# Attention with a row maximum sent unnegated, and the last denominators inverted in the output stage

## The reference

```python
x = x + L0(x, cond)                          # state-space layer, not touched
# L1(x, styles), 16 heads of width 32:
q, k, v = heads(q_flat), heads(k_flat), heads(v_flat)   # projections of the normalised x
attn = einsum('bhqd,bhkd->bhqk', q, k) * scale
attn = softmax(attn, axis=-1)
out = einsum('bhqk,bhkd->bhqd', attn, v).reshape(B, S, H)
out = einsum('bsh,oh->bso', out, w_weight) * w_dc[:, None, :]
skip = einsum('bsh,oh->bso', v_flat, u_weight) * u_dc[:, None, :]
return x + out + skip
```

## Time and profile before

| | |
|---|---|
| median of 3 runs | 3419.26 us (3412.98 to 3421.17) |
| the profiled execution | 3420.78 us, of it span 3419.0 us |
| mean granted TensorE clock | 0.906 of full speed |
| TensorE busy | 3041.7 us, 89% of the span |
| VectorE busy | 2272.5 us, 66% |
| ScalarE busy | 1125.7 us, 33% |
| GpSimd busy | 1132.0 us, 33% |
| DMA | 420.83 MB, mean 123 GB/s |

### The profile page before, as it was taken

The page is one execution under the profiler, slowest core; times in us unless marked ns, Lnnn a source line. Parts: engine busy times, 40 slices in busy tenths (PEclk is TensorE's granted clock), DMA queues, the critical chain, the costliest instruction groups (busy, mean ns, idle before and its releaser), DMA issues. The chain is left out here.

```text
span 3419.0 us, 55607 instructions
## 1 busy us (share of the span) xinstructions
PE 3041.7 (89%) x20298; PEld 1427.7 (42%) x20298; DVE 2272.5 (66%) x3150; ACT 1125.7 (33%) x1944; POOL 1132.0 (33%) x462
## 2 busy tenths in 40 slices
PE   6888865599999999999966999977999999999979
PEld 2555554234444444444434666652332333322324
DVE  3766763488898898989834433437767777776614
ACT  3644542011111111111112212214655665655620
POOL 0111111113333333333302110004656666666630
PEclk9878865588999999999996999988999999998989
DMA  2233224535555555555533433345424344353354
GB/s 74 114 109 142 89 104 137 131 82 141 146 149 146 149 148 147 156 144 147 144 122 125 155 116 139 128 153 127 102 56 109 93 98 106 81 125 81 75 189 144
DMA packets 248555, 420.83 MB, mean 123 GB/s; under 512 B 51736, under 2 KB 117912, under 8 KB 242024
## 3 DMA queue, kind: packets, MB, share of 16 engines
q1 hardware_dynamic: 202344, 385.61, 39.1%
q10 hardware_dynamic: 46080, 33.57, 4.7%
HBM read 257.82 MB, written 160.98 MB: 122 GB/s over the span
## 5 line engine op out<-in xcount | busy, mean ns | idle before, releaser
L491 DVE CUSTOM_DVE_ANT_0 b_h<-b_h,b_bx,b_bounds_all 128x256 f32<-128x256 f32 x2048 | 966.0, 535 | 137.9 <-PE b_bx L604 137.8
L1348 POOL TENSOR_TENSOR e_pair_sum<-e_probs 128x2048 f32<-128x2048 f32 x128 | 585.8, 4576 | 509.7 <-PE e_banks L1203 294.5
L1211 DVE TENSOR_REDUCE e_half_max<-e_banks 128x4 f32<-128x2048 f32 x256 | 585.5, 2291 | 251.0 <-PE e_banks L1164 250.9
L1324 ACT ACTIVATE e_probs<-e_banks 128x512 f32<-128x512 f32 x1024 | 556.0, 595 | 409.8 <-PE e_banks L1178 409.8
L1178 PE MATMUL e_banks<-e_qs,e_ks 97*128 97x512 f32 x1024 | 395.5, 467 | 8.7 <-DMA e_qs<-e_neg_t 4.8
L614 PE MATMUL b_y_psum<-b_h,b_c_weights 128*32 128x128 f32 x8224 | 344.2, 287 | 3.3 <-ACT b_y_stage L654 3.3
L604 PE MATMUL b_bx<-b_x_moving,b_b_weights 24*128 24x512 f32 x1024 | 265.6, 514 | 54.0 <-DMA b_x_moving<-xn_parts 44.6
L1178 PEld LDWEIGHTS e_banks<-e_qs,e_ks 97*128 97x128 f32 x1024 | 160.1, 195 | 355.6 <-ACT e_probs L1324 295.2
L654 ACT COPY b_y_stage<-b_y_psum 128x128 f32<-128x128 f32 x256 | 68.1, 266 | 724.0 <-PE b_y_psum L614 721.4
L525 PE MATMUL b_gate<-b_w_gate,b_x_tile 128*128 128x512 f32 x512 | 302.4, 674 | 3.6 <-DMA b_w_gate<-in_w_in_t_dram 3.6
L1188 PE MATMUL e_banks<-e_probs,e_v 128*32 128x512 f32 x2048 | 291.7, 643 | 0.5 <-ACT e_probs L1324 0.4
(11 more groups left out here) (183 smaller groups left out, 3358.1 us busy)
## 6 DMA issues: line engine op xcount, KB each, us to landing
b_x_moving<-xn_parts SPq DMA_DIRECT2D x256, 128.0 KB
e_ks<-qk_parts SPq DMA_DIRECT2D x48, 512.0 KB, 7.8
e_qs<-qk_parts SPq DMA_DIRECT2D x96, 256.0 KB, 11.6
xn_full<-a_xn SPq DMA_DIRECT2D x32, 512.0 KB, 2.6
xn_parts<-a_hi SPq DMA_DIRECT2D x64, 256.0 KB, 2.4
xn_parts<-a_lo SPq DMA_DIRECT2D x64, 256.0 KB, 2.4
b_x_moving<-xn_parts SPq DMA_DIRECT2D x256, 64.0 KB
silu_gate<-b_sg ACTq DMA_DIRECT2D x64, 256.0 KB, 4.1
```

The lines of the kernel that those rows point to most:

```text
L491: return nc.vector._custom_dve(bass.dve_ops.TENSOR_ADD_SAT, **operands)
L1211: nc.vector.tensor_reduce(out=half_max[:, u // UNITS % 2, :, r // NH, r % NH], in_=(banks[:, u % 2 * GROUP:(u % 2 + 1) * GROUP] if u < FIR ...
L1324: nc.scalar.activation(probs[:, g % 4, h, :], p_exp[h % 2], ACT.Exp).then_inc(exps, 1)
L1348: nc.gpsimd.tensor_tensor(out=pair_sum[:, t % 2], in0=probs[:, (2 * t) % 4], in1=probs[:, (2 * t + 1) % 4], op=ALU.add).then_inc(paired, 1)
```

## The change

In the attention stage the negation and its semaphore go. The transpose writes `max_t`, and `send_max` sends that; the 97th row of the stacked keys is -1 where it was 1. The wait for the buffer's earlier sends moves from the negation to the transpose. `invert` stays for batches 0 to 2. For the last batch VectorE only waits for the key sums in the attention stage. The PSUM tensor is now allocated around both stages: the output stage inverts the denominators straight out of its eighth bank, as VectorE's first operation, and SyncE stores them there. The output stage's SyncE asks for x2 of 3 tiles, then batch 1, then waits for the reciprocal and stores it, and only then asks for the other five x2 and batches 2 and 3.

```diff
 def send_max(sp, m):
-            sp.wait_ge(max_row, START + m + 1)
+            sp.wait_ge(max_turned, START + m + 1)
...
-                sp.dma_start(dst.bitcast(f32), neg_t[half][block * 32:block * 32 + ROWS, :].bitcast(f32)).then_inc(max_in[half], 16)
+                sp.dma_start(dst.bitcast(f32), max_t[half][block * 32:block * 32 + ROWS, :]).then_inc(max_in[half], 16)
...
 def dve_row(dve, m):
...
-            nc.vector.transpose(max_t[half][:], row_max[half][:]).then_inc(max_turned, 1)
-            dve.wait_ge(max_turned, START + m + 1)
             if m >= 2:
                 dve.wait_ge(max_in[half], START + m // 2 * SENDS)
-            nc.vector.tensor_scalar(out=neg_t[half][:], in0=max_t[half][:], scalar1=-1.0, scalar2=None, op0=ALU.mult).then_inc(max_row, 1)
+            nc.vector.transpose(max_t[half][:], row_max[half][:]).then_inc(max_turned, 1)
...
                 store_o(sp, HALVES - 1)
-                store_rden(sp, BATCH - 1)
                 for i in range(SLOTS):
                     sp.wait_ge(raw_out[i], START + 16 * ((HALVES - 1 - i) // SLOTS + 1))
-                sp.wait_ge(rden_out, START + BATCH * RDENS)
+                sp.wait_ge(rden_out, START + (BATCH - 1) * RDENS)
...
-                    nc.vector.memset(ks[i][KROWS:STACK].bitcast(f32), 1.0).then_inc(cleared, 1)
+                    nc.vector.memset(ks[i][KROWS:STACK].bitcast(f32), -1.0).then_inc(cleared, 1)
...
-                invert(dve, BATCH - 1)
+                dve.wait_ge(key_sums, START + BATCH * LANES * NQ)
...
 def out_phase
-        po = [ctx.enter_context(nc.psum_tensor(f"f_po{i}", [P, MODEL], f32)) for i in range(4)]
+        po = [banks[:, i] for i in range(4)]; den = banks[:, 7]; rden = sb("rden", [P, 512])
...
-                for t in range(NQ):
+                for t in range(3):
                     load_x2(sp, t)
-                for b in range(1, BATCH):
-                    load_batch(sp, b)
+                load_batch(sp, 1)
+                sp.wait_ge(inverted, START + 1)
+                for h in range(P // HD):
+                    sp.dma_start(RD[BATCH - 1, h], rden[h * HD:h * HD + NH * NK, :]).then_inc(rden_out, 16)
+                for t in range(3, NQ):
+                    load_x2(sp, t)
+                load_batch(sp, 2)
+                load_batch(sp, 3)
+                sp.wait_ge(rden_out, START + P // HD * 16)
                 load_rd(sp, BATCH - 1)
...
+                nc.vector.reciprocal(out=rden[:], in_=den).then_inc(inverted, 1)
                 for t in range(TILES):
```

More of the change, by code:

```diff
@@ L1056, in _, with attention_phase @@
                 batches(dve, body)
-def attention_phase(nc, I, QK, V, OT, RD, WDC, w_out, w_row, mats):
+def attention_phase(nc, I, QK, V, OT, RD, WDC, w_out, w_row, mats, banks):
     GROUP = P // HD
@@ L1082, in attention_phase @@
         sb = lambda n, s, d=f32: ctx.enter_context(nc.sbuf_tensor("e_" + n, s, d))
-        pb = lambda n, s, d=f32: ctx.enter_context(nc.psum_tensor("e_" + n, s, d))
         sems = []
@@ L1096, in attention_phase @@
         max_t = [sb(f"max_t{i}", [P, 32]) for i in range(2)]
-        neg_t = [sb(f"neg_t{i}", [P, 32], f32r) for i in range(2)]
         probs = sb("probs", [P, 4, GROUP, HALFQ]); pair_sum = sb("pair_sum", [P, 2, GROUP, HALFQ])
         raw = sb("raw", [P, SLOTS, HALFQ]); rden = sb("rden", [P, HALFQ]); den = sb("den", [P, HALFQ]); rd = sb("rd", [P, 2, HALFQ])
-        banks = pb("banks", [P, 2 * GROUP, 512])
         p_max = banks[:, 0:GROUP]; p_exp = [banks[:, GROUP + i] for i in range(2)]
@@ L1105, in attention_phase @@
         max_in = [sem(f"max_in{i}") for i in range(NH)]
-        unit_scores = sem("unit_scores"); unit_max = sem("unit_max"); max_whole = sem("max_whole"); max_turned = sem("max_turned"); max_row = sem("max_row")
+        unit_scores = sem("unit_scores"); unit_max = sem("unit_max"); max_whole = sem("max_whole"); max_turned = sem("max_turned")
         scores = sem("scores"); exps = sem("exps"); products = sem("products"); paired = sem("paired"); key_sums = sem("key_sums")
@@ L1351, in _, with out_phase @@
                         scale_raw(pool, (batch - 1) * LANES + r // NQ * 2 + SCALE_AT[r % NQ])
-def out_phase(nc, I, OT, RD, X2, w, w_row, first, out):
+def out_phase(nc, I, OT, RD, X2, w, w_row, first, banks, out):
     with ExitStack() as ctx:
@@ L1361, in out_phase @@
         ot = [first[:].bitcast(f32)] + [sb(f"ot{i}", [P, NK, SEQ]) for i in range(1, BATCH)]; rd = sb("rd", [P, NK, SEQ]); x2 = sb("x2", [P, NQ, MODEL]); o = sb("o", [P, 4, MODEL])
-        po = [ctx.enter_context(nc.psum_tensor(f"f_po{i}", [P, MODEL], f32)) for i in range(4)]
+        po = [banks[:, i] for i in range(4)]; den = banks[:, 7]; rden = sb("rden", [P, 512])
         b_in = [sem(f"b_in{i}") for i in range(BATCH)]; x_in = [sem(f"x_in{i}") for i in range(NQ)]
         products = sem("products"); scaled = sem("scaled"); added = sem("added"); o_out = [sem(f"o_out{i}") for i in range(4)]
-        rd_in = sem("rd_in"); divided = sem("divided")
+        inverted = sem("inverted"); rden_out = sem("rden_out"); rd_in = sem("rd_in"); divided = sem("divided")
         TILES = BATCH * NQ
@@ L1407, in _ @@
                             pe.wait_ge(divided, START + k + 1)
-                        mm = nc.tensor.matmul(po[t % 4][:], ot[b][:, k, q * P:(q + 1) * P], w[:, k, :], start=(k == 0), stop=(k == NK - 1))
+                        mm = nc.tensor.matmul(po[t % 4], ot[b][:, k, q * P:(q + 1) * P], w[:, k, :], start=(k == 0), stop=(k == NK - 1))
                     mm.then_inc(products, 1)
@@ L1421, in _ @@
                         dve.wait_ge(o_out[t % 4], START + 16 * (t // 4))
-                    nc.vector.tensor_tensor(out=o[:, t % 4, :], in0=w_row[:, t // NQ, :], in1=po[t % 4][:], op=ALU.mult).then_inc(scaled, 1)
+                    nc.vector.tensor_tensor(out=o[:, t % 4, :], in0=w_row[:, t // NQ, :], in1=po[t % 4], op=ALU.mult).then_inc(scaled, 1)
                     if t:
@@ L1454, in build @@
         mats = ctx.enter_context(nc.sbuf_tensor("ef_mats", [P, 2 * NH, SEQ], f32r))
-        attention_phase(nc, I, QK, V, OT, RD, WDC, w_out, w_row, mats)
-        out_phase(nc, I, OT, RD, X2, w_out, w_row, mats, out)
+        banks = ctx.enter_context(nc.psum_tensor("ef_banks", [P, 8, 512], f32))
+        attention_phase(nc, I, QK, V, OT, RD, WDC, w_out, w_row, mats, banks)
+        out_phase(nc, I, OT, RD, X2, w_out, w_row, mats, banks, out)
 def kernel(**inputs):
```

## The result

The changed kernel takes 3384.2 us (median of 13 runs, 3362.98 to 3404.06), the kernel before, run on the same chip, 3415.95 us (13 runs, 3401.23 to 3441.26). The ratio is 0.9906, with an interval of 0.9881 to 0.9931: faster by 24 to 41 us. The profiled execution took 3385.69 us, of it span 3383.9; that is 35.1 us less than the span of before.

The account below looks back on a forecast made before the run. TensorE's waits and low clock, 93 us over 29 attention halves, were winnable; minus 20.8, 16 and 13.8 leaves 42.4, plus 1.4, 0.2, 0.5, minus 0.1 gives 44.4. From 3419.26 that is 3375 us, range 3358 to 3392.

Parts of the forecast that it names:

- What the negation costs: VectorE's row step: the negation sits until GpSimd's addition ends; without it 0.46 us instead of 3.0, the 1.39 us gaps go.
- Rival D: VectorE's row step: the wait for GpSimd passes to the transpose, only about 5 us won, 3414; chance 0.05.
- What is late next: First halves of groups 5-7, 9-11, 13, 14: TensorE waits 2.6 us each for the row maximum's send, 20.8 us.
- The low clock behind the waits: Halves after the eight send waits: the clock sinks each time, 2.0 us each, 16 us, bounds 0 to 35.
- its own sign: Test on the eight send waits: prediction wrong if the low clock after them costs other than 1.5 to 3 us.
- Rival C: Each of the eight send waits is followed by the longest low stretch seen, 4.4 us: 3394; chance 0.12.
- Rival B: The eight send waits of 2.6 us don't sink the clock: 16 us less, 3359; chance 0.13.
- E: Slower: the clock stays low far longer after the eight send waits; at 9 us each 3431; chance 0.04.
- The inversions: Inverting halves of batches 0 to 2: 3.0 us idle plus 1.6 low clock each, 13.8 us stay.
- The first half of group 0: Start of the attention stage: one more TensorE gap goes, worth 1.4 us.
- The last inversion and batch 1: Boundary and output stage: removing the last inversion gains 0.5 us, bounds 0 and 2.0; batch 1 sooner costs nothing.
- the sum's nothing: Output stage: asking for batch 1 sooner taken as 0, bounds -0.5 and +3; tile 0's store landing hardly moves.

Follow-up runs that it names:

- e1: The kernel before with only the negation removed from the row step and -1 in the stacked keys: 3380.3 us, ratio 0.9881.
- e3: The changed kernel with +1 in the keys and a negation of 16 columns ahead of the transpose: about 3442 us, one run.
- e5: The kernel before, negation kept, with GpSimd adding only 128 of each 512 columns of the pairs: 3332.08 us, one run.
- e6: The changed kernel with the second half's row maximum sent ahead of the inverse sums, still behind the next group's stacks: 3367.84 us, one run.
- e7: The changed kernel with only the keys' stacks (1.5 MB) ahead of the row maximum's send, queries and values behind it: 3340.27 us, ratio 0.9747.
- e10: e7 with the reciprocal in four pieces and batch 0's load ahead of the store of GpSimd's last scaled output: 3324.24 us, ratio 0.9700.
- e2: The changed kernel with the negation put back, so only the output stage's edits differ from the kernel before: 3421.59 us, ratio 1.0003.
- e11: The changed kernel with send after keys, inversion in pieces, output-stage loads between tiles and batch 0 sooner: 3306.01 us, ratio 0.9647.

## Why the prediction was right, and where it was off

The kernel is faster, and the measured 3384.2 us lie within the range of 3358 to 3392. The forecast of 3375 was 9 us too low: the profiles show a gain of 35.1 us, the medians one of 31.8, against 44.4 foretold. That the time is off by 9 us and not by 12.6 is luck: the forecast counted from 3419.26 us, and over 13 runs the kernel before has 3415.95. By its steps:

**What the negation costs.** Right. The transpose took 0.211 to 0.213 us in all 32 cases, no gap stands at a row's end, and VectorE waits for TensorE there. e1 shows the gain on its own, and e3 to e5 show from both sides that it is GpSimd's addition that the negation sat behind. Rival D (3414) is refuted.

**What is late next.** Right, in place and size. The same eight halves wait, 19.1 us in all against 8 x 2.6 = 20.8, and they end 28.1 to 30.1 us after the half's start. e6 and e7 show that this landing is set by the data ahead in the queue. A ninth wait, of 0.69 us in group 8, was not foretold.

**The low clock behind the waits: the term that was mis-sized.** I took 2.0 us for each of eight, 16 us. Seven of the eight waits were followed by it, and it cost 5.9, 3.0, 3.2, 4.4, 1.5, 2.9 and 4.2 us, 25.1 in all. That is 3.1 for each of the eight, outside the 1.5 to 3 us beyond which I had called the prediction wrong, and single cases ran from 0 to 5.9: on this step its own sign speaks against it. The halves behind the waits ran at 0.79 to 1.00, where I had put each near 0.94. The 2.0 was the mean over the low halves of before, most of them behind a gap of 1.39 us. The waits here are longer (1.48 to 3.44 us), and what followed was longer as well: five of the seven reach the 3.0 that only five of the 19 low halves had before. The one that went without was the shortest. The largest, 5.9 us in a half at 0.79, lies beyond the 4.4 that I had called the longest. e1 and e6 have the same eight waits at other lengths, and bear this out on the mean, though not case by case:

| kernel | a wait, mean us | the low clock behind it, mean us |
|---|---|---|
| e6 | 1.6 | 1.5 |
| after | 2.4 | 3.1 |
| e1 | 2.7 | 3.3 |

In before, the 26 gaps of 1.39 us had 1.2 us of low clock behind them on the mean, those without any counted in. As an estimate from these four profiles, some 1 us of low clock for each us waited would have been the better price: 21 us for the eight waits foretold. Rival C (4.4 us each, 35 us) was about as near as the forecast: 25.1 lies midway between 16 and 35. Rival B (none) is refuted, and E (7.5 each or more) was far off.

**The inversions.** 12.1 us against 13.8. The first of them in after:

```profile
2563.10 3.35 DVE L1227 RECIPROCAL e_rden<-e_den 128x512 f32<-128x512 f32 x1
2563.22 1.07 PE L1200 MATMUL ef_banks<-e_pair_sum,e_lanes 128*32 128x512 f32 x8 [0.20 <-DVE e_den L1223]
...
2568.66 0.51 PE L1161 MATMUL ef_banks<-ef_mats 32*128 32x512 f32 x4 [2.06 <-DVE e_half_max L1208]
```

The idle times are 0.20 and 2.06 us, where the earlier trace rows have 2.73 and 0.50: the reciprocal now holds up the next unit, as worked out, though for 2.26 us in all where the prediction has 3.0. The three halves take 2.4, 4.5 and 5.3 us beyond 26.67, not 4.6 each; the first had no low clock behind it, and the second holds the ninth wait for the send (0.69).

These three terms leave 56.3 us in the stretch instead of 50.6: the attention stage gained 35.9 us against 42.4. The other 0.8 of that difference is rounding: a half takes 26.67 us, not 8 x 3.33.

**The first half of group 0.** I had 1.4 us for its one gap, which was in truth 0.97 long. The gap went, but the half took 29.7 us where it took 28.9. TensorE comes into it at half clock in both kernels (0.50 in the 12 us ahead), and in after it stayed there longer: 0.80 over the half against 0.86. The first scores start 0.8 us later than before, where I had 0.2 us of gain; the stages ahead of attention, which the change doesn't touch, vary by more than that between profiles.

**The last inversion and batch 1.** TensorE's idle time at the boundary went from 10.6 to 10.2 us, 0.4 less (0.5 foretold), and from group 15's start to the output stage it is 0.9 us shorter. The covering load of batch 0 set that end, as e10 shows. In the output stage I had foretold that tile 0's store would be issued 1 to 3 us later and land about when it did. It was issued 14.8 us after TensorE's start instead of 13.2 and landed at 37.5 instead of 36.2; TensorE's stall grew from 6.8 to 8.7 us. The stage as a whole took 127.2 us against 127.1, since less low clock followed the longer stall (6.8 us of it, 10.2 in before). So the sum's nothing held in this profile partly by luck: e2 has a stage of 131.6 us, 1.5 beyond the bound of +3, and the stall is longer in all seven profiles with this output stage.

**The spread.** After's runs lie between 3363 and 3404 us, with mean clocks of 0.917 down to 0.904; the longer ones have the lower clock. That is a wider stretch than the range that I had given for 8 in 10. How much of it comes from the eight waits is not shown: e11, whose profile has no such wait and a clock of 1.00 in all 29 halves, spreads from 3291 to 3320 us as well, with clocks of 0.927 to 0.918, and the stages ahead of attention vary by over 20 us between profiles. The 25.1 us are those of one execution. e1 has 6.6 us more in its stretch, 2.8 of it in longer waits, 1.6 in low clock behind them, and 2.2 in the second inverting half.

## What to carry to other kernels

A tiny step on a critical engine can cost ten times its work when it is held up by another engine's instruction (0.18 and 2.53 us here): compare its duration where the neighbour is idle with the duration where it isn't, and look at whether the two end together. Before a gap is counted as won, ask what comes in late as soon as the stretch is shorter; here a transfer behind 3.5 MB of loads took back 44 us of some 80, and placing it behind 1.5 MB gave these back. Where an idle time of TensorE is left over, price it by itself and by the low clock behind it together, with the second from waits of the same length, not from shorter ones.

## What the runs showed of the hardware that was not expected

- The multiplication by a scalar from SBUF to SBUF waits for GpSimd's addition with 16 and 17 columns (2.76 us) and with 32 (2.53 us) alike; it takes 0.18 us without the addition. I had expected 17 to be free.
- Low clock behind an idle time of TensorE comes unevenly: behind waits of 1.48 to 3.44 us it cost from nothing to 5.9 us, and the order of the costs is not that of the waits (2.24 us was followed by 5.9, 3.44 by 1.5). On the mean of eight waits it cost 0.9 to 1.3 us for each us waited, in after, e1 and e6.
- Four small DMAs can hold SyncE for 9.2 us when some MB are queued ahead (1.96 us in e7, where they are issued later, behind the sends), so what stands behind them in SyncE's program is late through the issue as well as through the transfer.
- Four transfers of a few KB, begun 5 us sooner behind the same 3.5 MB and issued to the last 2 us sooner, landed only 0.8 us sooner on the mean (e6); with 1.5 MB ahead of them they landed at 19.2 to 20.3 us instead of 28.1 to 30.1 (e7).
